# Gated cross-attention block: where each SBUF tile begins within 128 bytes

## The reference

```
x = x + tanh(g_xattn) * xattn(layernorm(x), ctx)
x = x + tanh(g_ffn)   * ffn(layernorm(x))

xattn: q = query @ Wq.T + bq;  k = ctx @ Wk.T + bk;  v = ctx @ Wv.T + bv
       scores = q k^T / 16; all but the 32 largest of each row become -inf
       out = softmax(scores) @ v @ Wo.T + bo
ffn:   relu(h @ W1 + b1) @ W2 + b2         (256 -> 1024 -> 256)
```

## Time and profile before

| | |
|---|---|
| median of three runs | 255.15 us |
| profiled execution | 255.62 us |
| its span | 252.8 us |
| TensorE matmul / weight load busy | 248.3 / 216.9 us |
| DVE / ACT / POOL busy | 186.0 / 136.0 / 170.4 us |
| DMA | 17.21 MB, mean 68 GB/s |

### The profile page before, as it was taken

How to read it: one execution, slowest core, us unless ns; L and a number is a source line. 1 busy time by engine, 2 the same in 40 slices (tenths; PEclk the granted TensorE clock), 3 DMA queues, 4 the chain that set the end, 5 groups by cost and what they waited for, 6 DMA issues and landing times.

```text
span 252.8 us, 4726 instructions
## 1 busy us (share of the span) xinstructions
PE 248.3 (98%) x1470; PEld 216.9 (86%) x1470; DVE 186.0 (74%) x784; ACT 136.0 (54%) x292; POOL 170.4 (67%) x224
## 2 busy tenths in 40 slices
PE   8999999999999999999999999999999999999995
PEld 7867799999999988898889888898889888988884
DVE  3699999989998992689887988977556967332024
ACT  2479585676757476336650475526561485135620
POOL 3377988897967699674679457773869367745640
PEclk9999999999999999999999999999999999999999
DMA  6993010080201000009012400110011000000202
GB/s 188 386 413 155 0 30 22 1 293 8 117 4 41 0 4 19 23 10 334 34 41 86 126 0 3 41 43 3 0 43 41 3 1 7 35 3 0 83 0 83
DMA packets 6872, 17.21 MB, mean 68 GB/s; under 512 B 800, under 2 KB 2368, under 8 KB 6592
## 3 DMA queue, kind: packets, MB, share of 16 engines
q1 hardware_dynamic: 6848, 16.93, 18.5%
HBM read 12.44 MB, written 4.19 MB: 66 GB/s over the span
## 4 chain that ended last, share of the span: by engine, by line
PE 93%; DVE 5%; issue 1%; ACT 0%; DVEq 0%
PE y_ps L492 24%; PE z_ps L477 12%; PE y_ps L499 12%; PE z_ps L478 12%; PE z_ps L479 12%; PE sc_ps L403 6%; PE pt_ps L424 3%; PE att_ps L445 1%; PE att_ps L444 1%; PE att_ps L442 1%; PE att_ps L458 1%; PE att_ps L443 1%; PE y_ps L305 1%; PE pt_ps L458 1%; DVE picked L1231 1%; PE z_ps L312 1%
## 5 line engine op out<-in xcount | busy, mean ns | idle before, releaser
L1618 POOL TENSOR_TENSOR hid_lo<-hid,hid_hi 128x512 fp32r<-128x512 f32 (+1 forms) x80 | 85.2, 1077 | 52.6 <-ACT hid L957 52.2
L492 PE MATMUL y_ps<-w_both,hid_hi 128*128 128x512 f32 x256 | 83.7, 402 | 0.0
L956 ACT ACTIVATE hid_hi<-z_ps,small_in 128x512 fp32r<-128x512 f32 (+1 forms) x80 | 48.2, 603 | 50.1 <-PE z_ps L479 49.4
L477 PE MATMUL z_ps<-x2nt_hi,w_hi 128*128 128x512 f32 (+1 forms) x160 | 57.1, 357 | 0.0
L478 PE MATMUL z_ps<-x2nt_lo,w_hi 128*128 128x512 f32 (+1 forms) x160 | 55.7, 348 | 0.0
L479 PE MATMUL z_ps<-x2nt_hi,w_lo 128*128 128x512 f32 (+1 forms) x160 | 55.6, 348 | 0.0
L499 PEld LDWEIGHTS y_ps<-w_both,hid_lo 128*128 128x128 f32 x248 | 46.6, 188 | 9.5
L499 PE MATMUL y_ps<-w_both,hid_lo 128*128 128x256 f32 x248 | 52.5, 281 | 0.0
L1289 DVE SCALAR_TENSOR_TENSOR x<-y_ps,tanh_g,x 128x256 f32<-128x256 f32 x64 | 26.8, 477 | 34.2 <-PE y_ps L499 33.1
L957 ACT ACTIVATE hid<-z_ps,small_in 128x512 f32<-128x512 f32 (+1 forms) x80 | 47.9, 599 | 0.0
L492 PEld LDWEIGHTS y_ps<-w_both,hid_hi 128*128 128x128 f32 x256 | 42.8, 188 | 4.4 <-DVE x L1289 0.3
(11 more groups left out here) (147 smaller groups left out, 357.5 us busy)
## 6 DMA issues: line engine op xcount, KB each, us to landing
x_ring<-x SPq DMA_DIRECT2D x8, 512.0 KB, 5.9
out<-x SPq DMA_DIRECT2D x15, 256.0 KB, 2.0
xt_in<-x_t SPq DMA_DIRECT2D x7, 512.0 KB, 4.7
w_in<-w SPq DMA_DIRECT2D x2, 1024.0 KB, 10.4
wkq_in<-w_kq SPq DMA_DIRECT2D x1, 514.0 KB, 3.5
wvo_in<-w_vo SPq DMA_DIRECT2D x1, 513.0 KB, 6.5
xt_in<-x_t SPq DMA_DIRECT2D x2, 256.0 KB, 5.9
ctx_in<-ctx_t SPq DMA_DIRECT2D x1, 462.0 KB, 9.5
```

The lines of the kernel that those rows point to most:

```text
L477: mm(dst, w1_hi[:, k, cols], hi[:, k, toks], start=k == 0, stop=False)
L492: last = mm(y_ps[t % 3][:], hid_hi[:, q % RING, tile_of_unit(g, j)], w2_both[:, c, :], start=c == 0, stop=c == KF - 1)
L956: func(hid_hi[:, q % RING, cols], z_ps[q % 2][:, cols], ACT.Relu, bias=b1[:, c:c + 1]).then_inc(hid_hi_made, 1)
L1618: nc.gpsimd.tensor_tensor(hid_lo[:, q % RING, cols], hid[:, q % FULL_RING, cols], hid_hi[:, q % RING, cols], ALU.subtract).then_inc(hid_lo ...
```

## The change

The calls of `sb` are put in another order, and one tile `half_line` of 64 bytes that nobody uses is added. Tiles whose size is a multiple of 128 bytes come first. Behind `half_line` come the tiles that TensorE streams as f32r: `vals_hi`, `vals_lo`, `vals_rest`, `w2_both`, `x2nt_hi`, `x2nt_lo`. Last come the tiles of other sizes. Names that are views of a tile (`wk`, `b1` and so on) are made at the end; they are the same slices. Nothing else differs.

```diff
--- before.py
+++ after.py
@@ -4,6 +4,7 @@
 
 B, T, S, D, F = 4, 1024, 154, 256, 1024
 P = 128
+LINE = 128
 TILES = 4
 GROUP = TILES * P
 GROUPS = B * T // GROUP
@@ -60,15 +61,9 @@
 
         hid_lo = sb("hid_lo", [P, RING, GROUP], f32r)
 
-        wk_in, wq_in = wkq_in[:, :, 0:D + 1], wkq_in[:, :, D + 1:2 * (D + 1)]
-        ctx_in = sb("ctx_in", [P, KD, B * S])
-        wvo_in = sb("wvo_in", [P, KD, 2 * D + 1])
-        bk_bq = sb("bk_bq", [P, KD])
         mt = sb("mt", [P, KD, D])
-        key_bias = sb("key_bias", [P, KD + 1])
 
         wo_bv = sb("wo_bv", [P, KD, D])
-        neg_mean = sb("neg_mean", [P, 1])
         ones_row = sb("ones_row", [1, P], f32r)
         vo_bias_hi = sb("vo_bias_hi", [P, D], f32r)
         vo_bias_lo = sb("vo_bias_lo", [P, D], f32r)
@@ -81,18 +76,45 @@
         w1_in = sb("w1_in", [P, KD, F])
         w2_in = sb("w2_in", [P, KF, D])
         x_ring = sb("x_ring", [P, X_RING, TILES * D])
-        small_in = sb("small_in", [P, 2 + KF + 2 * D])
-        wk, bk = wk_in[:, :, 0:D], wk_in[:, :, D:D + 1]
-        wq, bq = wq_in[:, :, 0:D], wq_in[:, :, D:D + 1]
-        wv, wo_t, bv = wvo_in[:, :, 0:D], wvo_in[:, :, D:2 * D], wvo_in[:, :, 2 * D:2 * D + 1]
-        b1 = small_in[:, 2:2 + KF]
-        bo = small_in[:, 2 + KF:2 + KF + D]
-        b2 = small_in[:, 2 + KF + D:2 + KF + 2 * D]
 
         ident = sb("ident", [P, P])
         ones = sb("ones", [P, P])
+
+        wvo = sb("wvo", [P, KD, D])
+        vo_bias = sb("vo_bias", [P, D])
+
+
+        values = sb("values", [P, B + 2, D])
+        stacked = sb("stacked", [96, B - 1, D])
+        w1_hi = sb("w1_hi", [P, KD, F], f32r)
+        w1_lo = sb("w1_lo", [P, KD, F], f32r)
+        b2_pair = sb("b2_pair", [P, 2, D])
+
+        xt_in = [sb(f"xt_in_{i}", [P, KD, GROUP]) for i in range(2)]
+        top = sb("top", [P, TILES, TOPK])
+        picked = sb("picked", [P, TILES, 2 * P])
+        pt_hi = sb("pt_hi", [P, 2, 2 * P], f32r)
+        pt_lo = sb("pt_lo", [P, 2 * P], f32r)
+
+
+        x2 = [sb(f"x2_{i}", [P, TILES, D]) for i in range(2)]
+        x2n = sb("x2n", [P, TILES, D])
+        sb("half_line", [P, LINE // 8])
+        vals_hi = sb("vals_hi", [P, B, D], f32r)
+        vals_lo = sb("vals_lo", [P, B, D], f32r)
+        vals_rest = sb("vals_rest", [P, B, D], f32r)
+        w2_both = sb("w2_both", [P, KF, 2 * D], f32r)
+        w2_hi, w2_lo = w2_both[:, :, 0:D], w2_both[:, :, D:2 * D]
+        x2nt_hi = [sb(f"x2nt_hi_{i}", [P, KD, GROUP], f32r) for i in range(2)]
+        x2nt_lo = [sb(f"x2nt_lo_{i}", [P, KD, GROUP], f32r) for i in range(2)]
+
+        ctx_in = sb("ctx_in", [P, KD, B * S])
+        wvo_in = sb("wvo_in", [P, KD, 2 * D + 1])
+        bk_bq = sb("bk_bq", [P, KD])
+        key_bias = sb("key_bias", [P, KD + 1])
+        neg_mean = sb("neg_mean", [P, 1])
+        small_in = sb("small_in", [P, 2 + KF + 2 * D])
         neg_half = sb("neg_half", [P, TILES])
-
         tanh_g = sb("tanh_g", [P, 2])
         keys = sb("keys", [P, KD, B * S])
         score_bias = sb("score_bias", [P, B * S])
@@ -100,43 +122,24 @@
         mt_mean = sb("mt_mean", [P, KD, 2])
         u_col = sb("u_col", [P, KD])
         rest_row = sb("rest_row", [1, P])
-        wvo = sb("wvo", [P, KD, D])
-        vo_bias = sb("vo_bias", [P, D])
-
-
-        values = sb("values", [P, B + 2, D])
-        vals_hi = sb("vals_hi", [P, B, D], f32r)
-        vals_lo = sb("vals_lo", [P, B, D], f32r)
-        vals_rest = sb("vals_rest", [P, B, D], f32r)
-        stacked = sb("stacked", [96, B - 1, D])
-        w1_hi = sb("w1_hi", [P, KD, F], f32r)
-        w1_lo = sb("w1_lo", [P, KD, F], f32r)
-        w2_both = sb("w2_both", [P, KF, 2 * D], f32r)
-        w2_hi, w2_lo = w2_both[:, :, 0:D], w2_both[:, :, D:2 * D]
-        b2_pair = sb("b2_pair", [P, 2, D])
-
         stats1 = sb("stats1", [P, TILES, 6])
         mv1 = [sb(f"mv1_{i}", [P, TILES, 2]) for i in range(2)]
         norm1 = [sb(f"norm1_{i}", [P, 2, TILES]) for i in range(2)]
-        xt_in = [sb(f"xt_in_{i}", [P, KD, GROUP]) for i in range(2)]
         score = sb("score", [P, TILES, S])
-        top = sb("top", [P, TILES, TOPK])
         neg_max = sb("neg_max", [P, TILES])
         left = sb("left", [P, TILES, S])
         probs = sb("probs", [P, TILES, S])
-        picked = sb("picked", [P, TILES, 2 * P])
         inv_denom = sb("inv_denom", [P, TILES])
-        pt_hi = sb("pt_hi", [P, 2, 2 * P], f32r)
-        pt_lo = sb("pt_lo", [P, 2 * P], f32r)
-
-
-        x2 = [sb(f"x2_{i}", [P, TILES, D]) for i in range(2)]
         stats2 = sb("stats2", [P, TILES, 6])
         mv2 = sb("mv2", [P, TILES, 2])
         norm2 = sb("norm2", [P, 3, TILES])
-        x2n = sb("x2n", [P, TILES, D])
-        x2nt_hi = [sb(f"x2nt_hi_{i}", [P, KD, GROUP], f32r) for i in range(2)]
-        x2nt_lo = [sb(f"x2nt_lo_{i}", [P, KD, GROUP], f32r) for i in range(2)]
+        wk_in, wq_in = wkq_in[:, :, 0:D + 1], wkq_in[:, :, D + 1:2 * (D + 1)]
+        wk, bk = wk_in[:, :, 0:D], wk_in[:, :, D:D + 1]
+        wq, bq = wq_in[:, :, 0:D], wq_in[:, :, D:D + 1]
+        wv, wo_t, bv = wvo_in[:, :, 0:D], wvo_in[:, :, D:2 * D], wvo_in[:, :, 2 * D:2 * D + 1]
+        b1 = small_in[:, 2:2 + KF]
+        bo = small_in[:, 2 + KF:2 + KF + D]
+        b2 = small_in[:, 2 + KF + D:2 + KF + 2 * D]
 
         z_ps = [bank("z_ps0"), bank("z_ps1")]
         y_ps = [bank("y_ps0"), bank("y_ps1"), bank("y_ps2")]
```

## The result

The kernel after takes 253.36 us (median of 7 runs, 253.16 to 254.19) where the kernel before took 255.15 beside it: ratio 0.9929, 95% interval 0.9908 to 0.9950. Measured twice more (experiment 5), the same kernel gave 0.9971 (0.9953 to 0.9988) and 0.9944 (0.9925 to 0.9964). The change is a gain of 0.3 to 0.7%, by these medians 0.8 to 1.8 us. I had forecast 247.8 us, 7.4 less. The direction held; at least three quarters of the gain was not there.

A forecast was written before the change was run, and what follows sets the result against it. TensorE's matmul spacing was taken to bound the kernel. Of a 13.3 us full f32r gain, 5/8 gave 8.3, less 0.9 lost before 80 us: 7.4 us off the 255.15 us median, 247.8 us, 8-in-10 range 242 to 257.

The forecast's parts named there:

- TensorE's slots set the time, and nothing takes over: Whole kernel: TensorE busy 248.3 of 252.8 us, so only matmul spacing moves the time; no other engine becomes the limit.
- The edits costed at nothing: Two-pass f32 matmuls, DVE, ACT, POOL and DMAs: their tiles move too, but the new offsets were claimed to cost nothing.
- The good end, 8 ns for a 256 and 16 for a 512, of which 5/8: All f32r matmuls: full gain 13.3 us, from the value-bias product's 273 ns against 281; 5/8 taken, 8.3 us.
- The loss per 512 is recoverable: 512-column f32r matmuls: slots of 233 ns claimed to lose up to 16 ns each, 544 x 16 = 8.7 us at full gain.
- my estimate of 14.4 us from that page: All f32r matmuls: losses of 17.2 ns per 512 and 8.8 per 256 against the skill's issue-gap rule, to be had.
- The start of the stream counts, distance does not: f32r streams: starts at odd multiples of 32 bytes claimed slow, multiples of 64 fast; load-stream distance alone frees no long stream.
- Layer one's 256s are the row with the gain already in it: Layer one's 256-column matmuls: 276 ns records, load and stream already 64 apart, taken to show 5 of the 8 ns.
- half of my 1.85 us: Work before 80 us: TensorE gains 1.85 us, of which 0.9 us is let go because POOL and DVE are nearly full.
- Rival 1: All f32r matmuls: nothing changes, the loss is the stream's own limit wherever it begins; 255.15 us give or take 1; chance 0.30.
- Rival 2: Only load-stream distance counts: layer two's 256s and attention's short products go from 281 to 276 ns; 253.4 us; chance 0.12.
- Rival 3: Slower: load and stream cross block boundaries together, 3 ns per 256 and 6 per 512, 5.0 us; 260.2 us; chance 0.16.

The follow-up runs named there:

- experiment 5: Kernel after remeasured twice: 0.9971, 0.9944 of before; kernel after with common load-stream distance changed to 0, 16, 224 bytes: 0.9983, 1.0024, 1.0007.
- experiment 1: TensorE alone, no computation: f32r streams and loads at remainders 0, 32, 64, 96 of 128; 512-column slots 226.7 ns at distance 0, 229.1 at 192, 233.5 at 64.
- experiment 3: Kernel after with the unused tile 192 bytes instead of 64, so distance modulo 256 is 64 instead of 192: 255.08 us, 0.9985 of before.
- experiment 4: Kernel before with parts of the change: layer one's distance alone to 192, 255.60 us (1.0009); w2_both alone moved, 254.81 us (0.9979).
- experiment 6: TensorE alone: loads of 128 to 32 columns, and the kernel's mixture at distances in steps of 16; mixture's mean slot 196.9 ns at 192, 199.3 at 64.

## Why the prediction was wrong, point by point

- *TensorE's slots set the time, and nothing takes over.* Right: 1.54 us of slots, 1.59 us of stretch, same waits, same POOL and DVE.
- *The edits costed at nothing.* Right: L406 296, L356 379, POOL 1299, MAX8 306.
- *The good end, 8 ns for a 256 and 16 for a 512, of which 5/8.* This is the step that failed. It measured 0.39 and 2.59 ns. The good end came from the record of `vo_bias_lo`, 273 ns, less the 163 of the steady chains. But record less slot is 161 to 163 only where matmul follows matmul in one kind. The timeline of the kernel before around that product:
```profile
28.91 0.38 PE L385 MATMUL y_ps<-vo_bias_hi,ones_row 1*128 1x256 f32 x1
29.13 0.27 PE L386 MATMUL y_ps<-vo_bias_lo,ones_row 1*128 1x256 f32 x1
29.34 0.39 PE L477 MATMUL z_ps<-x2nt_hi,w_hi 128*128 128x256 f32 x1
```
Its slot is some 205 ns (29.34 - 29.13 in rounded figures), not 110: it stands at a switch of kinds. Nor was `vo_bias_lo` the only f32r stream from a multiple of 64: the product from `vo_bias_hi` ahead of it is one too, and its record is 0.38 us. Single records of it vary, too, 277 and 276 ns in the first trace of the kernel after, 277 and 273 in the third. The start of the next matmul would have struck the row out.
- *The loss per 512 is recoverable.* Most of it is not, in any pattern run. The Trainium skill (page TensorE: Matmul & The Clock Gate, section Back-to-back issue gap) gives N / 2.4 + 2.5 ns, 215.8 and 109.2, as the isolated gap of a warm matmul, without setting f32r apart. No steady f32r run here was under 226.7 or 113.3, so my estimate of 14.4 us from that page had 544 x 10.9 + 576 x 4.1 = 8.3 us in it that no placement run here gives.
- *The start of the stream counts, distance does not.* Wrong way round (experiments 1 and 3). I had dismissed distance because layer one's 512s ran at 233 ns with stream and load "already 64 apart". They were 64 apart modulo 256 before and 192 after. Modulo 128, which the wording of the change suggests, the two are equal, so I read as unchanged what the change improved most: layer one's 512s.
- *Layer one's 256s are the row with the gain already in it.* They were good because of distance 64, in a kernel the best for 256s (116.26 over the whole of experiment 3), and the change took it from them: 116.0 to 116.8, at the start 114 to 117. The layer-one part of experiment 4 shows it alone: at 192, beside their own loads, they went from 116.0 to 117.4. That is also why nothing is gained before 78 us: 165 of these slots lose 0.15 us there, about what all other f32r slots gain. That half of my 1.85 us is lost there to DVE and POOL was never put to the test.
- *The rivals.* Rival 1 (the stream's own limit) was right for the larger part, the floor of 226.7 under the 232.5 of before. Rival 2 named the right variable and 253.4 us, which is what came; but it put the gain into the 256s of layer two and attention (5 ns each), and it lies in the 512s (2.6 ns each). Its time is a coincidence. Rival 3 wanted layer two's 256s over 282; they are at 279.
- The Trainium skill (page SBUF — State Buffer, section SBUF: two separate sides) has TensorE wait for no other engine. The runs agree to within 1 ns a slot: 229.1 ns alone, 229.9 in the kernel. Lines of 16 bytes don't account for what was seen between a stream and the load beside it: distances that are all multiples of 16 read 226.7 to 234.3.

Open: what in the chip has a period of 256 bytes between the stream and the load, why a smaller load doesn't free a 512, why starts off a multiple of 32 cost in the sweep, and how the order of kinds turns the settled values into those of a kernel. The runs give the table, not the mechanism.

## What to carry to other kernels

Where a kernel is bound by f32r matmuls, compare start-to-start slots in unbroken chains, not records, and lay out all streamed tiles at one remainder of 256 and all loaded tiles at another: 192 between them won 2.6 ns of 233 here. One common distance is not enough by itself: 64, 0 and 224 won 0.65, 0.53 and 0.04 of the 1.6 us by the stretch, and layer one's pair moved alone won nothing. Before a single row is taken as the good end of a range, read the start of the next instruction. And take remainders modulo more than the number that the change names.

## What the runs showed of the hardware that was not expected

- A steady f32r stream took 17/16 cycles a column at best (226.7, 113.3 ns), and the slot depends on load less stream modulo 256 bytes, by up to 7.6 ns of 227; operands that both start 4 bytes further cost up to 239.
- After idling, the first slots of 512 columns took 427 ns, 512 columns at 1.2 GHz, while the granted clock of that stretch reads 1.00. Windows of the program of experiment 6, at its start and later (the count of matmuls in 2 us is in brackets behind PE's busy time, the granted clock the last but two):
```profile
10.00:12.00 2.00, 2.00 (x5) 1.61 (x6) 0.00 (x0) 0.00 (x0) 0.00 (x0) 1.00 0.00 0
...
20.00:22.00 2.00, 2.00 (x10) 1.65 (x10) 0.00 (x0) 0.00 (x0) 0.00 (x0) 1.00 0.00 0
```
What the distance costs at 2.4 GHz did not show at 1.2. The last products of experiment 1, one partition of `sc` against `wa` at distance 64, with a granted clock of 0.5:
```profile
127.62 7.02 PE L62 MATMUL ps<-sc,wa 1*128 1x512 f32 x16
134.45 3.61 PE L62 MATMUL ps<-sb,wb 1*128 1x256 f32 x16
```
Sixteen slots take 6.83 us, 427 ns each, 512 columns at 1.2 GHz with nothing added. With all 128 partitions, at distance 128, slots 2 to 7 of the same program read 426 and 427 as well.
